# Aligned operands and split products in the dense layers of a graph network block

## The reference

```
S = (adj + adj.T) / 2 + I;  d = rowsum(S) ** -0.5;  A = d[:, None] * S * d[None, :]
x = x + (adj @ A) @ relu(layernorm(x))
h = relu(layernorm(x))
Wh[k] = h @ W[k]                                     # 8 heads of 64
att[k] = softmax(where(adj > 0, leaky_relu(src + dst, 0.2), -9e15))
enc = concat_k elu(att[k] @ Wh[k])                   # 2048 x 512
o1 = relu(enc @ W1.T + b1)                           # 256
o2 = relu(o1 @ W2.T + b2)                            # 128
o3 = relu(o2 @ W3.T + b3)                            # 256
x = x + o3 @ W4.T + b4                               # 512
```

## Time and profile before

| | us |
|---|---|
| median of 3 runs (884.63 to 884.87) | 884.76 |
| the profiled execution | 884.79 |
| its span, first to last instruction | 882.9 |
| TensorE (PE) busy | 855.8 |
| VectorE (DVE) busy | 691.6 |
| ScalarE (ACT) busy | 414.5 |
| GpSimd (POOL) busy | 276.5 |

### The profile page before, as it was taken

One profiled execution on the slowest core, in us unless ns is written; L12 is line 12 of the kernel. 1 busy time (PEld: TensorE's weight loads), 2 busy tenths in 40 slices (PEclk: granted clock), 3 DMA queues, 4 the chain that ended last, 5 costly groups with the idle time before them and its releaser, 6 DMA issues.

```text
span 882.9 us, 15244 instructions
## 1 busy us (share of the span) xinstructions
PE 855.8 (97%) x5145; PEld 751.5 (85%) x5145; DVE 691.6 (78%) x1188; ACT 414.5 (47%) x758; POOL 276.5 (31%) x293
## 2 busy tenths in 40 slices
PE   2999999999999999999799999999999999999998
PEld 1878888888888888878699999999999999999663
DVE  6789986556557775686999989999999999999722
ACT  3445433321111122345576666666666666775431
POOL 0000000000000000066738555555555655575222
PEclk9999999999999999999799999999999999999999
DMA  9959922603332321040160000000000032001033
GB/s 349 407 218 373 367 95 77 185 0 119 97 99 90 107 99 54 22 171 4 27 219 16 20 24 26 26 24 24 25 26 24 24 96 72 14 1 49 28 120 140
DMA packets 36117, 87.37 MB, mean 99 GB/s; under 512 B 7072, under 2 KB 7968, under 8 KB 36064
## 3 DMA queue, kind: packets, MB, share of 16 engines
q1 hardware_dynamic: 35024, 82.46, 26.7%
q0 software_dynamic: 1040, 4.26, 1.3%
HBM read 73.93 MB, written 12.78 MB: 98 GB/s over the span
## 4 chain that ended last, share of the span: by engine, by line
PE 90%; DVE 8%; DMA 1%; ACT 1%; issue 0%; ACTq 0%; DVEq 0%
PE bank L1578 25%; PE bank L73 15%; PE bank L75 15%; PE bank L74 15%; PE bank L1604 13%; DVE l_q L1227 3%; PE bank L2036 3%; PE bank L1998 1%; DVE e L859 1%; PE bank L2019 1%; PE bank L2028 1%; DMA l_h<-x 1%; DVE l_stats L784 1%; DVE x_lo L855 1%; PE bank L923 0%
## 5 line engine op out<-in xcount | busy, mean ns | idle before, releaser
L1227 DVE SCALAR_TENSOR_TENSOR l_q<-bank,neg_d,mask 128x512 fp32r<-128x512 f32 x512 | 338.7, 742 | 24.4 <-PE bank L1578 24.1
L1578 PE MATMUL bank<-l_parts,l_q 128*128 128x260 f32 x2048 | 252.0, 284 | 3.8 <-DVE l_q L1227 3.8
L1578 PEld LDWEIGHTS bank<-l_parts,l_q 128*128 128x128 f32 x2048 | 249.3, 190 | 4.3 <-issue 3.9
L73 PE MATMUL bank<-x_hi,s_hi 128*128 128x512 f32 x448 | 174.5, 389 | 0.0
L75 PE MATMUL bank<-x_hi,s_lo 128*128 128x512 f32 x448 | 174.3, 389 | 0.0
L74 PE MATMUL bank<-x_lo,s_hi 128*128 128x512 f32 x448 | 174.3, 389 | 0.0
L746 POOL TENSOR_TENSOR l_prod<-wh,l_a 128x512 f32<-128x512 f32 x30 | 36.3, 1229 | 389.0 <-ACT wh L718 389.0
L1351 ACT ACTIVATE l_mask<-mask 128x512 fp32r<-128x512 uint8 (+1 forms) x256 | 136.4, 619 | 0.1
L1604 PE MATMUL bank<-l_parts,l_mask 128*128 128x260 f32 x1024 | 128.8, 286 | 0.7 <-DVE l_parts L1233 0.7
L1604 PEld LDWEIGHTS bank<-l_parts,l_mask 128*128 128x128 f32 x1024 | 127.0, 189 | 1.0 <-ACT l_o_q L1357 0.9
L75 PEld LDWEIGHTS bank<-x_hi,s_lo 128*128 128x128 f32 x448 | 84.1, 188 | 17.6
(11 more groups left out here) (180 smaller groups left out, 1086.1 us busy)
## 6 DMA issues: line engine op xcount, KB each, us to landing
rows<-adj_t SPq DMA_DIRECT2D x48, 512.0 KB, 3.9
l_now<-adj SPq DMA_DIRECT2D x16, 512.0 KB, 7.5
l_rows_k<-adj_t SPq DMA_DIRECT2D x16, 512.0 KB, 8.3
l_src<-e_rows SPq DMA_DIRECT2D x30, 256.0 KB, 3.2
l_kept<-adj SPq DMA_DIRECT2D x12, 512.0 KB, 13.2
wh_store<-wh POOLq DMA_DIRECT2D x1, 4160.0 KB, 15.8
l_h<-x SPq DMA_DIRECT2D x4, 1024.0 KB, 17.4
x<-x SPq DMA_DIRECT2D x1, 4096.0 KB, 13.5
```

Source lines behind the costliest of these rows:

```text
L73: pe.matmul(acc, hi, rhs_hi, start=first, stop=False, skip_group_check=True)
L1227: v.scalar_tensor_tensor(out=q[:, i, :], in0=bank[S_BANKS[hh]][:], scalar=neg_d[:, i, h:h + 1], in1=mask[:, i, cols], op0=ALU.is_ge, op1=A ...
L1578: return pe.matmul(bank[Q_BANKS[hh][t]][:, 0:PW], q[:, i, t * P:(t + 1) * P], parts[pair_slot][:, hh, i, :], start=i == 0, stop=i == T - 1)
```

## The change

It does the following.

1. Fillers (352 bytes ahead of the early buffers and of `l2_w`, 96 ahead of `l5_w1_hi`, 192 ahead of the new dense weights) bring the two operands of every product of 512 columns to equal remainders by 512 bytes: 480 in the first two stages, 320 in the dense layers.
2. The four blocks of `parts` are ordered anew, both heads of a tile in one row of 520 columns, so that the mask phase reads one run of 260 columns.
3. In the first stage, `guard(4)` goes ahead of `statistics(1)`, `cut_lo(5)` ahead of `variances(1)`, and ScalarE's cuts 5 to 8 ahead of square roots. In the projection the norms of the second half are made one turn sooner.
4. The second, third and fourth dense layers are made from parts as the first is, six products for two. Their weights are cut in the last round of attention (ScalarE, then GpSimd). Of each layer's output ScalarE makes the high part and, in place in PSUM, the whole; VectorE makes the rest, for two of the twenty GpSimd (`other_rests`).
5. The third chunk is stored in four transfers; the second layer of the last chunk goes one row sooner; GpSimd's bias for later chunks waits for the first finished row instead of the last normalisation; the last rows use the banks of the first layer.

The core of the diff:

```
+W_SHIFT = 48
+SCRATCH = 512
+EARLY_SHIFT = 88
+W1_SHIFT = 24
...
         degree(4)
+        guard(4)
         statistics(1)
-        guard(4)
+        cut_lo(5)
         variances(1)
-        cut_lo(5)
...
         keep_first_part()
+        cut_hi(5)
         take_root(4)
         take_ln_root(1)
-        cut_hi(5)
+        cut_hi(6)
         take_root(5)
-        cut_hi(6)
         normalise(1, 4, 6)
+        cut_hi(7)
         take_root(6)
-        cut_hi(7)
         normalise(1, 6, 8)
-        take_root(7)
         cut_hi(8)
         cut_x_hi(8)
+        take_root(7)
...
+        sb("l2_to_w_hi", [P, EARLY_SHIFT])
         w_hi = sb("l2_w_hi", [P, KC, F], F32R)
...
-            for k in in_turns(T, (cut_turned, 0), (reduce_e, 2)):
+            def late_chain(t, b):
+                if t == 4:
+                    variances(1)
+                if t == 5 or t == 6:
+                    for n in range(3 * t - 15, 3 * t - 12):
+                        late_norms(n)
+            for k in in_turns(T, (cut_turned, 0), (late_chain, 0), (reduce_e, 2)):
...
-        A_HI, C_HI, C_LO, A_LO = (slice(k * HE, (k + 1) * HE) for k in range(4))
-        BOTH_C = slice(HE, 3 * HE)
+        A_HI, A_LO, C_HI, C_LO = range(4)
+        FIRST = ((0, 6), (1, 6), (2, 2), (3, 2))
+        BOTH_C = slice(2 * HE, 6 * HE)
...
-            nc, ctx, [("l4_parts0", [P, 2, T, PW], F32R)],
+            nc, ctx, [("l4_parts0", [P, T, 2 * PW], F32R)],
...
-                                         parts[pair_slot][:, hh, i, :], start=i == 0, stop=i == T - 1)
+                                         parts[pair_slot][:, i, hh * PW:(hh + 1) * PW], start=i == 0, stop=i == T - 1)
...
-                                         parts[pair_slot][:, :, i, BOTH_C], start=i == 0, stop=i == T - 1)
+                                         parts[pair_slot][:, i, BOTH_C], start=i == 0, stop=i == T - 1)
...
+                        if not more and r == LAST:
+                            a.wait_ge(q_ready, T * (2 * LAST + 1) + MASK_TILES)
+                            for dst, src_w in ((w2_hi, w2_s), (w3_hi, w3_s), (w4_hi, w4_s)):
+                                a.activation(dst[:], src_w[:], ACT.Copy).then_inc(w_hi_ready, 1)
...
+                        if not more and r == LAST:
+                            p.wait_ge(w_hi_ready, 4)
+                            for dst, src_w, hi in ((w2_lo, w2_s, w2_hi), (w3_lo, w3_s, w3_hi), (w4_lo, w4_s, w4_hi)):
+                                p.tensor_tensor(dst[:], src_w[:], hi[:].bitcast(F32), ALU.subtract
+                                                ).then_inc(w_lo_ready, 1)
                         first_head()
...
-                p.wait_ge(dense.last_enc_ready, T - GT * EARLY)
-                for c in range(1, CHUNKS):
-                    dense.add_bias(p, c)
+                p.wait_ge(dense.out_ready, 1)
+                dense.add_bias(p, 1)
+                dense.add_bias(p, 2)
+                dense.other_rests(p)
+                dense.add_bias(p, 3)
...
-        step = 1 if c == self.NCH - 1 else self.GT
+        step = 1 if c >= self.NCH - 2 else self.GT
...
     def relu3(self, a, c, m):
+        acc = self.bank[self.SUM3_BANKS[m]][:]
         a.wait_ge(self.sum3_done, self.K3 * c + m + 1)
-        a.activation(self.o3[:, c % 2, m, :], self.bank[self.SUM3_BANKS[m]][:], ACT.Relu, bias=self.b3_s[:, m:m + 1]
-                     ).then_inc(self.o3_ready, 1)
+        a.activation(self.o3[0][:, c % 2, m, :], acc, ACT.Relu, bias=self.b3_s[:, m:m + 1]).then_inc(self.o3_ready, 1)
+        a.activation(acc, acc, ACT.Relu, bias=self.b3_s[:, m:m + 1]).then_inc(self.o3_ready, 1)
...
+    def rest3(self, v, c, m):
+        v.wait_ge(self.o3_ready, 2 * (self.K3 * c + m) + 2)
+        v.tensor_tensor(self.o3[1][:, c % 2, m, :], self.bank[self.SUM3_BANKS[m]][:],
+                        self.o3[0][:, c % 2, m, :].bitcast(F32), ALU.subtract).then_inc(self.rest_ready, 1)
...
     def sum_row(self, pe, c, t):
+        acc, (hi, lo), (w_hi, w_lo) = self.row_bank(c, t), self.o3, self.w4
...
         for k in range(self.K3):
-            pe.wait_ge(self.o3_ready, self.K3 * c + k + 1)
-            mm = pe.matmul(self.bank[self.ROW_BANKS[t % 2]][:], self.o3[:, c % 2, k, t * P:(t + 1) * P],
-                           self.w4_s[:, k, :], start=k == 0, stop=k == self.K3 - 1)
+            pe.wait_ge(self.o3_ready, 2 * (self.K3 * c + k) + 1)
+            pe.matmul(acc, hi[:, c % 2, k, of_tile], w_hi[:, k, :], start=k == 0, stop=False, skip_group_check=True)
+            pe.matmul(acc, hi[:, c % 2, k, of_tile], w_lo[:, k, :], start=False, stop=False, skip_group_check=True)
+        for k in range(self.K3):
+            self.wait_for_rest(pe, 3, c, k)
+            mm = pe.matmul(acc, lo[:, c % 2, k, of_tile], w_hi[:, k, :], start=False, stop=k == self.K3 - 1,
+                           skip_group_check=True)
```

More of the change, by code:

```diff
@@ L993, in spread_and_project, with attend_and_finish @@
                 stored, fac_ready)
-def attend_and_finish(nc, before, bank, wh, e, mask, ident, adj, e_rows, fac, neg_d, wh_store, x1_store, weights, out):
+def attend_and_finish(nc, before, bank, wh, e, mask, ident, adj, e_rows, fac, neg_d, wh_store, x1_store, weights, weight_parts, out):
     with ExitStack() as ctx:
@@ L1018, in attend_and_finish, with of_head, of_sums @@
         PW = 4 * HE
-        A_HI, C_HI, C_LO, A_LO = (slice(k * HE, (k + 1) * HE) for k in range(4))
-        BOTH_C = slice(HE, 3 * HE)
+        A_HI, A_LO, C_HI, C_LO = range(4)
+        FIRST = ((0, 6), (1, 6), (2, 2), (3, 2))
+        BOTH_C = slice(2 * HE, 6 * HE)
+        def of_head(which, head):
+            first, step = FIRST[which]
+            start = (first + step * head) * HE
+            return slice(start, start + HE) if isinstance(head, int) else bass.ds(start, HE)
+        def of_sums(which, hh):
+            start = of_head(which, hh).start - hh * PW
+            return slice(start, start + HE)
         Q_BANKS = ((0, 1, 2, 3), (2, 3, 4, 5))
@@ L1289, in _, with rests_between @@
                                 ).then_inc(retry_chain, 1)
-                dense.elu_chunk(v, CHUNKS - 1)
+                dense.rest1(v, 1, 0)
+                for m in range(K3):
+                    dense.rest3(v, 0, m)
+                dense.average_tile(v, second)
+                def rests_between(of, c):
+                    if c < CHUNKS - 2:
+                        of.rest2(v, c)
+                        of.rest1(v, c + 1, 0)
+                    for m in range(K3):
+                        of.rest3(v, c, m)
                 def finish_chunk(of, c):
+                    if c + 1 < CHUNKS:
+                        of.rest1(v, c + 1, 1)
                     of.finish_row(v, c, 0)
@@ L1300, in finish_chunk @@
                         of.take_lo(v, c + 2, 3)
+                    if c == CHUNKS - 2:
+                        of.rest2(v, CHUNKS - 1)
                     of.finish_row(v, c, 2)
+                    if c == CHUNKS - 2:
+                        for m in range(K3):
+                            of.rest3(v, CHUNKS - 1, m)
                     of.finish_row(v, c, 3)
-                for c in range(CHUNKS - 2):
-                    finish_chunk(dense, c)
+                finish_chunk(dense, 0)
+                dense.average_tile(v, second + 1)
+                dense.elu_tile(v, second)
+                dense.average_tile(v, second + 2)
+                dense.rest2(v, 1)
+                dense.elu_tile(v, second + 1)
+                dense.average_tile(v, second + 3)
+                dense.elu_tile(v, second + 2)
+                dense.rest1(v, 2, 0)
+                dense.elu_tile(v, second + 3)
+                for m in range(K3):
+                    dense.rest3(v, 1, m)
+                finish_chunk(dense, 1)
                 v.wait_ge(fine_counted, 1)
@@ L1310, in _ @@
                 with if_set(v, retry):
+                    for m in range(K3):
+                        dense.rest3(v, CHUNKS - 2, m)
                     finish_chunk(dense, CHUNKS - 2)
@@ L1461, in serve_layers @@
                                 of.take_hi(a, c + 2, k)
+                        if first and c == 0:
+                            of.exp_tile(a, last + 1)
                     of.relu2(a, CHUNKS - 1)
@@ L1659, in dense_layers @@
                             of.turn(pe, c + 2, 1)
+                        else:
+                            of.sum2(pe, c + 1)
                         of.sum_row(pe, c, 1)
@@ L1868, in store, with wait_for_rest, whole_to @@
                 "(t p) f -> p t f", p=P), self.res[c % 2][:, t:t + step, :])
-            done.then_inc(self.last_stored if step == 1 else self.stored[c % 2], 16)
+            done.then_inc(self.stored[c % 2], 16)
     def wait_for_stores(self, sp):
-        for b in range(2):
-            sp.wait_ge(self.stored[b], 16 * ((self.NCH - b) // 2))
-        sp.wait_ge(self.last_stored, 16 * self.GT)
+        sp.wait_ge(self.stored[0], 16 * (self.NCH // 2 - 1 + self.GT))
```

(19 more changed lines are left out.)

215 lines of the change are left out of this document (131 added, 84 removed), and 4 rows, old and new, of the table RESTS.

## The result

The changed kernel takes 875.34 us (median of four runs, 873.72 to 876.47) against 884.82 (884.63 to 884.90): a ratio of 0.9891, with a 95% interval of 0.9875 to 0.9908. The forecast was 872.6, in a range of 869.5 to 877.5. The runs of the changed kernel lie 2.75 us apart, those of the kernel before 0.27; what spreads them is told with the experiments.

What follows compares the result with a forecast made beforehand. The prediction took TensorE's matmul issue plus a few waits as the bound. Early products 1.4, projection 1.1, norms 1.2, mask phase 2.8 and dense layers 5.7 sum to 12.2; 884.79 - 12.2 = 872.6 us, range 869.5 to 877.5.

Steps and rivals of the forecast that it cites:

- Early products: First stage: 187 matmuls go from 0.2342 to 0.2265 us at equal remainders, one wait included; saves 1.4 us (0 to 1.7).
- The rival that addresses don't matter: Early, projection and dense products: something else than addresses makes the early ones slow; 876.3 us, chance 0.17.
- Projection: Projection stage: 192 products 5 to 6 ns shorter save 1.1 us; earlier norms remove TensorE waits, 1.2 us.
- Mask phase: Attention: one run of 260 columns brings 7.87 us to 7.69, 15 rounds, 2.8 us; rival of no gain 875.4, chance 0.10.
- the lower bound: Mask phase in attention: gain 0 if the 3 ns come from something else, such as a start off 16 bytes.
- Last round of attention: Attention's end: ScalarE's three weight cuts and GpSimd's three rests fit into idle time; cost 0.
- Clock: Rival: new waits in the dense layers lower TensorE's granted clock; 890.6 us, slower than before, chance 0.03.
- Dense layers: Dense layers: six products for two and equal remainders save 9.2 us, new waits cost 3.5; net 5.7.
- rests come late: Rival: dense layers bound by ScalarE pass, pass, VectorE rest; 7 us of waits instead of 3.5, 876.1 us, chance 0.13.
- Storing by tile: Third chunk stored in four pieces: three more issues on SP, last store begins when the last row is done; 0.
- The product at 47.11 us: First stage: this product waits some 0.3 us for a VectorE rest; the new order saves that wait.
- the upper bounds together: Whole kernel: all upper bounds at once, with 8.2 of the dense layers, give 869.1 us.

Runs made afterwards that it cites:

- e2: The changed kernel with the early tiles and W's parts back at remainder 128 by 512 bytes: 876.60 us.
- e8: The changed kernel with early tiles and W's parts at remainder 224 (other operand 480), first dense layer's weights at 448 (encodings 320): 876.75 us.
- e9: The changed kernel with the first stage's VectorE and ScalarE order and the place of the second half's norms as before the change: 879.09 us.
- e3: The changed kernel with the whole tile of the parts beginning 8 bytes later: 877.10 us.
- e10: The kernel before the change plus three unused GpSimd subtractions (256, 256 and 1024 columns) ahead of its last combination: 887.14 us.
- e1: The changed kernel with GpSimd's three rests of the weights behind the first half of its last combination: 873.86 us.
- e4: The changed kernel with the largest rest of the weights made in four pieces of 256 columns, at the old place: 872.48 us.
- e5: The changed kernel with GpSimd's three rests of the weights behind its whole last combination, TensorE waiting for each before the layer that reads it: 872.34 us.
- e11: e5 with two of six row products left out (those with the rests of W4); run once: 870.2 us.
- e6: The changed kernel with the third chunk stored in one transfer, as before the change: 876.16 us.

## Why the prediction was right, and where it failed

The size and the sign were right, with 875.34 in the range; the forecast was 2.7 us too low, and 3.8 in the profiled run. That it came so near is in part luck: 4.95 us lost at two places that were priced at nothing and 1.3 too much for the mask phase stand against 2.05 too little for the dense layers and 0.5 for the projection. Without the 2.05 the profiled run would have taken 878.4 us, outside the range. By its own terms:

- **Early products: 1.4 forecast, 1.19 measured.** The reason holds for the products (e2, e8). With as many slow first products as the kernel before (10, not 12) the stage would have given some 1.6. What the sum missed is that the new addresses and the new order need each other: with the addresses alone (e9) a wait of 1.06 us eats nearly the whole gain, 47.18 us against 47.45, and with the order alone (e2) the stage takes 46.65 (slow first products: 9 in e9, 8 in e2). The address rule was too narrow: an equal remainder by 256 bytes is enough, which the traces of before could not tell. The rival that addresses don't matter is out, and with it the inference from the Trainium skill's two independent read ports (page "TensorE: Matmul & The Clock Gate", section "Step-by-step: what each phase is for"): on this point the measured 0.227 and 0.234 us decide.
- **Projection: 2.3 forecast, 2.81 measured,** from two errors against each other. The products gave some 0.5 instead of 1.1 (e2, with W's parts at the old remainder, takes 0.50 longer; by kind the products went from 235, 232 and 234 to 236, 228 and 232 ns). An equal remainder did not bring 0.227 here, and no run shows why. The norms gave 2.3 instead of 1.2 (e9), as no rest came late in place of the three waits.
- **Mask phase: 2.8 forecast, 1.53 measured.** The term was mis-sized: a product went from 0.1230 to 0.1214 us, not to 0.1201. The step "the streamed columns, weights and banks are otherwise alike" left out the start by 16 bytes, which the prediction had itself named for the lower bound; e3 shows that it holds the other half. Whether the first half came from joining the two runs or from the start's move from 4 to 8 past a multiple of 16, no run separates.
- **Last round of attention: 0 forecast, 3.85 lost.** This is the step that failed. "It has idled 5.37 us before that one's second half, so nothing is late" counted GpSimd's own time and its readers, not what VectorE does meanwhile. The row was there: VectorE's step of 1.11 us beside GpSimd had been read for the projection and as a rival in the dense layers, and not carried to this place. e10 shows the loss without the rest of the change, e1, e4 and e5 how it goes. The Trainium skill has the rule, on the page "SBUF — State Buffer", section "Who interferes with whom": VectorE and GpSimd share a pair of ports as an exclusive lock, for a whole instruction, when VectorE reads two tensors of SBUF or runs a tensor_scalar in a two-port mode. The traces agree: 2.03 us for 32 columns, 2.35 for the average, and 0.69, unchanged, for rests that read PSUM; in which mode the step on 32 columns ran no view says.
- **Clock.** The rival had it in the dense layers, where it stayed at 1.00. It fell to 0.50 where no wait had been forecast, around the end of 2.4 us of idling, and not every time.
- **Dense layers: 5.7 forecast, 7.75 measured.** The gain of 9.2 fits the distances (227 ns a product, as forecast), so that what is missing, 1.45, is what the waits cost instead of 3.5; added up from start to start, TensorE's gaps come to 2.1 us, the longest 0.65 from one product to the next (840.35). ScalarE's passes of 0.69 us start every 0.57: the four behind a third layer, counted as 2.76, take from 821.04 to 823.44, and VectorE's rest follows 0.03 later, not 0.2. e11 shows that the rival "rests come late" was near all the same. e8 prices the first layer's addresses at 0.46 us (63.12 against 62.66, 0.6 forecast); no run takes back the products from parts alone, so that their share rests on the counted distances.
- **Storing by tile: 0 forecast, and 1.1 us behind the last row were lost,** but not to the four stores (e6). "The last store begins when the last row is done" holds; it ended later in every kernel whose rows come sooner. Why stays open.
- **Two slips in the working.** The product at 47.11 us starts 0.41 us after the one before it, a wait of some 0.18, not 0.3; and the upper bounds together give 869.3, not 869.1. Neither moves the forecast.

## What to carry to other kernels

When work is moved to an idle engine, ask not only whether that engine has time and who waits for its result, but what runs beside it: here a long GpSimd instruction on SBUF held a VectorE step that reads two tiles of SBUF, or a tensor_scalar on it, to its end. Put such work beside VectorE steps that read PSUM, or cut it into pieces that are shorter than the slack. Try the two operands of a long series of fp32r products at equal remainders by 256 bytes (two of three groups of products gained 5 to 7 ns each by it, the third some 2), and streamed columns that begin at a multiple of 16. When products become quicker, look again at the orders of the engines that feed them: a wait that was hidden can take the gain.

## What the runs showed of the hardware that was not expected

- Operands 256 bytes apart by 512 are as quick as equal ones (226 to 227 ns for 512 columns of fp32r); 128 or 160 apart cost 4 to 8 ns (early products and first dense layer; the projection's products stayed at 228 to 236).
- A streamed operand of 260 columns costs 1.6 to 1.9 ns more when it begins 8 bytes past a multiple of 16 (7.77 / 64 and 15.58 / 128 against 15.34 / 128 and 7.67 / 64 us). Its distance from the other operand changes by the same 8 bytes, and no run tells the two apart.
- With the same 2.3 to 2.5 us of idling TensorE's granted clock fell from 1.00 to 0.50 in seven of nine profiled runs and stayed in two, worth 1.4 to 1.7 us here.
- Fetches of instructions of 16 KB ran within the last 5.4 us for up to 2.5 us, beside the last stores. The Trainium skill, page "Advanced Engine Details and Errata", section "ISA Cache", gives 16 KB as the cache line. The trace agrees: the page of the kernel after has, in its DMA queues (packets, MB, share), 0.46 MB in 28 packets.

```profile
q8 instruction: 28, 0.46, 0.2%
```
